# Message passes: the last tile's two matmuls on 64 rows each, its second feature half and its matrix rows held at the upper partitions too

## The reference, cut to what matters

```python
def _spmm(src, dst, w, x, n):
    return jax.ops.segment_sum(w[:, None] * x[src], dst, num_segments=n)
# layer 0: two of these
agg = _spmm(src, dst, edge_weight, x, n)
h = (x + agg) @ W + b
x = jax.nn.gelu(_layer_norm(h, g, be), approximate=False)
# layer 1: one, with a weight of 1 for each edge, scaled by 1 / sqrt(degree)
msg = h[src] * norm[:, None]
out = jax.ops.segment_sum(msg, dst, num_segments=n_nodes)
```

## Time and profile before

| | us |
|---|---|
| median of 3 executions | 1819.25 |
| lowest, highest | 1815.8, 1825.24 |
| the profiled execution's own time | 1821.75 |
| its span in the profile | 1820.0 |

### The profile page before, as it was taken

How to read it: one execution, slowest core, us unless ns; L and a number is a source line. 1 busy time by engine, 2 the same in 40 slices (tenths; PEclk the granted TensorE clock), 3 DMA queues, 4 the chain that set the end, 5 groups by cost and what they waited for, 6 DMA issues and landing times.

```text
span 1820.0 us, 30944 instructions
## 1 busy us (share of the span) xinstructions
PE 1697.8 (93%) x10117; PEld 1359.8 (75%) x10118; DVE 946.7 (52%) x1613; ACT 569.3 (31%) x854; POOL 187.2 (10%) x263
## 2 busy tenths in 40 slices
PE   6999999888889999999999999999999999998995
PEld 4898888888776777777777777766677777787784
DVE  7999999998873301111034444643413143345446
ACT  3135677788890000000011111234400000004442
POOL 4000000000001100000000000000000000153683
PEclk9999999999999999999999999989999999999998
DMA  4103344454459544445434434900064434434375
GB/s 98 1 23 135 135 165 187 200 214 202 196 239 352 166 146 142 138 148 162 146 117 121 127 121 122 242 36 1 18 207 152 135 108 126 144 122 130 105 243 180
DMA packets 136919, 261.73 MB, mean 144 GB/s; under 512 B 22236, under 2 KB 74735, under 8 KB 136606
## 3 DMA queue, kind: packets, MB, share of 16 engines
q1 hardware_dynamic: 116824, 237.02, 40.2%
q0 software_dynamic: 5808, 14.70, 2.2%
q10 hardware_dynamic: 14230, 9.29, 1.7%
HBM read 161.13 MB, written 108.09 MB: 148 GB/s over the span
## 4 chain that ended last, share of the span: by engine, by line
issue 56%; PE 29%; ACT 7%; DVE 4%; ACTq 1%; POOL 1%; DMA 1%; DVEq 1%; SPq 0%; POOLq 0%
PE ps L2143 12%; PE ps L2174 6%; ACT wide L878 4%; PE ps L2144 4%; ACT ps L822 3%; PE ps L2395 2%; PE ps L2379 2%; DVE act_c L1385 1%; PE ps L2042 1%; PE ps L2387 1%; PE ps L2371 1%; ACTq L865 0%; PE ps L2191 0%; PE ps L2203 0%; ACTq L822 0%
## 5 line engine op out<-in xcount | busy, mean ns | idle before, releaser
L2174 PE MATMUL ps<-wide 128*128 128x320 f32 (+1 forms) x2000 | 533.2, 427 | 0.0
L2174 PEld LDWEIGHTS ps<-wide 128*128 128x128 f32 x2000 | 378.3, 190 | 141.3 <-ACT act_c L1001 0.3
L2143 PE MATMUL ps<-early,act_c 128*128 128x200 bf16 x2400 | 299.3, 254 | 46.7 <-ACT ps L822 30.2
L2143 PEld LDWEIGHTS ps<-early,act_c 128*128 128x128 bf16 x2400 | 222.7, 98 | 61.6 <-issue 60.0
L2174 PE MATMUL ps<-wide,act_a 128*128 128x320 f32 (+1 forms) x1000 | 264.4, 426 | 2.3 <-ACTq L910 1.7
L2174 PEld LDWEIGHTS ps<-wide,act_a 128*128 128x128 f32 x1000 | 189.8, 190 | 75.6 <-DMA wide<-weight_matrix 2.1
L878 ACT COPY wide<-ps 128x832 f32<-128x832 f32 x200 | 169.8, 849 | 131.5 <-PE ps L2144 129.7
L822 ACT ACTIVATE ps<-wide 128x832 f32 (+1 forms) x200 | 173.4, 868 | 40.6 <-ACT wide L878 33.3
L1385 DVE TENSOR_TENSOR act_c<-act_a,pair_tab 128x3072 bf16<-128x3072 bf16 x98 | 169.8, 1752 | 21.3 <-PE ps L2144 21.3
L1513 DVE TENSOR_TENSOR wide<-ps,rows 128x1280 f32<-128x1280 f32 x10 | 14.9, 1490 | 283.5 <-PE ps L2191 283.5
L2143 PE MATMUL ps<-act_a,act_c 128*128 128x200 bf16 x1152 | 140.4, 251 | 13.5 <-issue 7.1
(11 more groups left out here) (264 smaller groups left out, 1794.7 us busy)
## 6 DMA issues: line engine op xcount, KB each, us to landing
wide<-weight_matrix SPq DMA_DIRECT2D x90, 800.0 KB, 4.5
wide<-count_matrix SPq DMA_DIRECT2D x45, 800.0 KB, 4.5
weight_matrix<-wide SPq DMA_DIRECT2D x60, 480.0 KB, 2.5
count_matrix<-wide SPq DMA_DIRECT2D x60, 480.0 KB, 2.6
weight_matrix<-wide SPq DMA_DIRECT2D x20, 560.0 KB, 2.7
count_matrix<-wide SPq DMA_DIRECT2D x20, 560.0 KB, 2.7
wide<-weight_matrix SPq DMA_DIRECT2D x20, 400.0 KB, 3.8
routed_tokens<-in_x_dram SPq DMA_DIRECT2D x2, 3072.0 KB, 28.6
```

What stands on the lines that cost most here:

```text
L2143: nc.tensor.matmul(weights, hot_parts[:, slot % PART_SLOTS, part, two, :, k], hot_key[mask_slot][:, mask_two, 0:WCOLS, k], start=False, st ...
L2174: i = nc.tensor.matmul(ps[:, 2 * sub + h, 0:n], features[:, q * QUADS + t, h * P:(h + 1) * P], moving, start=q == 0 and t == 0, stop=q == ...
```

## The change

In tile 24 only the lower 53 rows hold nodes, so 64 rows are enough for a matmul. For this tile the matmul h = 0 now uses partitions 0 to 63, and h = 1 uses partitions 64 to 127. For that the second feature half of tile 24 must lie at partitions 64 and up too (`double_tail`, a DMA within SBUF issued by ACT, 53 rows of 512 bytes, once for each pass), and the tile's 64 matrix rows are written twice to DRAM (`TAIL_ROWS`, two more DMAs by SP for each unit and matrix, 64 rows of 640 bytes each), which makes the four pieces 6 tiles each. PE gets one more wait in each pass, ahead of the first sub-block's last tile. A semaphore is saved by joining `moe_w1_loaded` and `moe_w2_loaded`.

```diff
-PIECES = (slice(0, 7), slice(7, 13), slice(13, 19), slice(19, 25))
-STORED = 16 * len(PIECES)
+HALF_ROWS = P // 2
+PIECES = (slice(0, 6), slice(6, 12), slice(12, 18), slice(18, 24))
+TAIL_ROWS = (slice(0, HALF_ROWS), slice(HALF_ROWS, P))
+STORED = 16 * (len(PIECES) + len(TAIL_ROWS))
...
# SP, write(u2, half, n)
                 sp.dma_start(matrix[ds(u2, 1), half, :, tiles, :].rearrange("a p t c -> (a p) t c"),
                              stage[half][:, first_row + tiles.start:first_row + tiles.stop, :]).then_inc(written[half], 16)
+                if tiles.stop == TILES - 1:
+                    for part in TAIL_ROWS:
+                        sp.dma_start(matrix[ds(u2, 1), half, part, TILES - 1, :].rearrange("a p c -> (a p) c"),
+                                     stage[half][0:HALF_ROWS, first_row + TILES - 1, :]).then_inc(written[half], 16)
...
# ACT, after the weight loads and the waits behind them
+            def double_tail(features):
+                act.dma_start(features[HALF_ROWS:HALF_ROWS + LAST, TILES - 1, P:D], features[0:LAST, TILES - 1, P:D]).then_inc(tail_doubled, 16)
+
             def take_sums(k, s, sub):
...
+            act.wait_ge(input_normed, UNITS)
+            double_tail(act_a)
             super_blocks(act, first_layer, gelu_first)
+            act.wait_ge(gelu_done, 1 + SUPERS)
+            double_tail(act_b)
...
             gcn_operand(SUPERS - 1)
+            act.wait_ge(gcn_in, SUPER + SUPERS * SUPER)
+            double_tail(act_b)
...
# PE, stream(k, s, sub, q)
                 for t in range(QUADS):
+                    tail = q == UNITS - 1 and t == QUADS - 1
+                    if tail and first_block:
+
+                        pe.wait_ge(tail_doubled, 16 * (k + 1))
                     for h in range(KD):
-                        moving = ring[:, q, :, t, :] if n == SUB else last_ring[:, q, t, 0:n]
-                        i = nc.tensor.matmul(ps[:, 2 * sub + h, 0:n], features[:, q * QUADS + t, h * P:(h + 1) * P], moving,
-                                             start=q == 0 and t == 0, stop=q == UNITS - 1 and t == QUADS - 1)
+                        part = slice(h * HALF_ROWS, (h + 1) * HALF_ROWS) if tail else slice(0, P)
+                        moving = ring[part, q, :, t, :] if n == SUB else last_ring[part, q, t, 0:n]
+                        i = nc.tensor.matmul(ps[:, 2 * sub + h, 0:n], features[part, q * QUADS + t, h * P:(h + 1) * P], moving,
+                                             start=q == 0 and t == 0, stop=tail)
```

More of the change, by code:

```diff
@@ L88 @@
 HALF = UGROUPS // 2
-PIECES = (slice(0, 7), slice(7, 13), slice(13, 19), slice(19, 25))
-STORED = 16 * len(PIECES)
+HALF_ROWS = P // 2
+PIECES = (slice(0, 6), slice(6, 12), slice(12, 18), slice(18, 24))
+TAIL_ROWS = (slice(0, HALF_ROWS), slice(HALF_ROWS, P))
+STORED = 16 * (len(PIECES) + len(TAIL_ROWS))
+assert LAST <= HALF_ROWS and PIECES[-1].stop == TILES - 1
 ACCS = 8
@@ L482, in build_program @@
         input_normed = sem("input_normed")
+        tail_doubled = sem("tail_doubled")
         degree_sums = sem("degree_sums")
@@ L508, in build_program @@
         gcn_in = sem("gcn_in")
-        moe_w1_loaded = sem("moe_w1_loaded")
-        moe_w2_loaded = sem("moe_w2_loaded")
+        moe_weights_loaded = sem("moe_weights_loaded")
         biases_loaded = sem("biases_loaded")
@@ L726, in _ @@
                         here_e = slice(e * D, (e + 1) * D)
-                        sp.dma_start(moe_w1[:, :, here_e], a["L1_ffn_w1"][e].rearrange("(k p) n -> p k n", p=P)).then_inc(moe_w1_loaded, 16)
-                        sp.dma_start(moe_w2[:, :, here_e], a["L1_ffn_w2"][e].rearrange("(k p) n -> p k n", p=P)).then_inc(moe_w2_loaded, 16)
+                        sp.dma_start(moe_w1[:, :, here_e], a["L1_ffn_w1"][e].rearrange("(k p) n -> p k n", p=P)).then_inc(moe_weights_loaded, 16)
+                        sp.dma_start(moe_w2[:, :, here_e], a["L1_ffn_w2"][e].rearrange("(k p) n -> p k n", p=P)).then_inc(moe_weights_loaded, 16)
                     sp.dma_start(moe_b1, a["L1_ffn_b1"].rearrange("e n -> (e n)").partition_broadcast(P)).then_inc(biases_loaded, 16)
@@ L2354, in _ @@
             message_pass(2, [0])
-            pe.wait_ge(moe_w1_loaded, 16 * MOES)
-            pe.wait_ge(moe_w2_loaded, 16 * MOES)
+            pe.wait_ge(moe_weights_loaded, 16 * 2 * MOES)
             def experts_at(first, parts):
```

## The result

The changed kernel takes 1845.32 us (median of 4 executions, 1840.96 to 1851.3) against 1819.31 for the kernel before in the same comparison: 26.0 us more. The ratio is 1.0145, 95% interval 1.012 to 1.0169. The forecast was 1840 in a range of 1829 to 1852.

A forecast was written before the change was run, and what follows sets the result against it. PE, busy for 93% of the span, was taken to bound the kernel. Profiled 1821.75 + 22.3 (wait) + 2.5 (clock) - 4 (halves) = 1842.5; that execution was 2.5 above the median, so 1840 us, range 1829 to 1852.

The forecast's parts named there:

- The spacing and the clean path: In a pass, time is PE's instructions times spacing (0.269 us at 320 columns); any added wait stays in full.
- The wait in pass 0: Before the first last tile PE waits for the copy behind ACT's weight loads: 22.3 us, bounds 19 to 29.
- 2.6 to 5.9: Bounds in us for landing pass 0's copy: a write in quiet, or the router's loads just ahead of it.
- The clock: After PE's stand in pass 0, 5 us at 1.2 GHz, half of it lost: 2.5 us, bounds 0 and 5.
- The halves beside each other: Last tiles' row halves run beside each other: 0.15 us saved per wide tile, 4 us over all 30.
- in sequence: Rival: last tiles' halves run one after the other, 12 us lost, 1856 with the stall; 8 in 100.
- strict program order: Rival: last tiles' records start strictly in program order, three slots for a tile, 8 us more, 1848; 8 in 100.
- switching isn't free: Last tiles: two switches cost 0.39 us; the rival, free switching with the stall, gives 1828, 7 in 100.
- The copies of passes 1 and 2: Free: features complete 14 us (pass 1) and 10 us (pass 2) before the last tile; uncovered, 3 to 6 each.
- The writes of stage 1: 80 more DMAs, 30 us of SP's queue, hidden by 419 us of SP waiting for ACT's copies: no cost.

The follow-up runs named there:

- the run on the same rows: Kernel before with the last tile's two matmuls both on partitions 0 to 63, no copies, waits or other writes: 1859.54 us, 1.006 times before.
- the wait alone: Kernel before with only the three copies and PE's three waits for them, last tile still on 128 rows: 1874.76 us, 1.0133 times before.
- the run with the copy by SP: Changed kernel with pass 0's copy issued by SP, ahead of its second sub-block loads, instead of by ACT: 1855.95 us, 1.0037 times the kernel before.
- the writes alone: Kernel before with six DMAs instead of four for each unit and matrix, nothing else: 1858.79 us, 1.0061 times before.
- x loaded twice: Changed kernel with x's last 53 rows loaded to partitions 0 and 64 instead of pass 0's copy and wait: 1854.92 us, 1.0023 times the kernel before.
- five DMAs: The kernel before with split writes only, the last tile's 128 rows in one DMA, five for each unit and matrix: 1854.59 us, one execution.
- the loads doubled: Kernel with x loaded twice, matrices written as before, SP loading the last tile's lower 64 rows twice into the ring: 1844.92 us, 0.997 times the kernel before.

## Why the prediction came out

**The spacing and the clean path** held: what was added to PE's queue in pass 0 stayed in full: 24.2 us until the record behind `degrees(0)` and none of it given back in the pass. In pass 2 it doesn't hold, as the run on the same rows shows (2.0 us of 3.9): the waits of the earlier trace rows end at 838, and PE has others there.

**The wait in pass 0** was the decisive step, and right in place, cause and size: 22.3 us forecast, 22.68 measured, 22.91 with the wait alone. Its terms: ACT free at 597.3 forecast, 600.5 measured. 2 us of that is the start of the loads (560.26; 558.3 forecast), from the later stage 1. The loads themselves took 40.3 us, 2.2 less than before, where 3.5 were forecast: a standing PE does free ACT's queue, by less. Since PE too came to its last tile 2.6 us late, the stand came out the same. That its size is right to 0.4 us is in part luck: the landing was forecast for 600.7 and came at 603.84, and the later stage 1 moved both its ends. The copy took 1.20 to issue and landed 3.0 after its issue began; 0.4 and then 3 were forecast. That a mere move to another queue would have met a new backlog (12.0 us to land) the prediction's "2.6 to 5.9" did not contain; the run with the copy by SP showed it.

**The clock** cost 1.7 us, 2.5 were forecast from a restart whose slow stretch lasted 5 us; here it lasted 3.5.

**The halves beside each other** were forecast from pairs of 64 columns, at 0.15 us for each tile; it is 0.14 to 0.145. The rivals fell on the record list: the halves start 0.007 us apart, so they neither run in sequence nor in strict program order, and the first record behind each switch comes 0.36 us after the one before it, so switching isn't free. The run on the same rows measured the two switches alone, 0.39, as worked out from the earlier trace rows. The rule of the Trainium skill (TensorEngine Tiling, Key Properties), that a change of tiling mode drains the engine, agrees with the 0.36 us here. Of its "up to 2x" 1.08 us against 0.93 is left, with 0.39 us for the two switches.

**The copies of passes 1 and 2** were free, as forecast: in the changed kernel neither pass shows a wait for one.

**The writes of stage 1** were the step that was mis-sized: "They are hidden by 419 us in which SP waits for ACT's copies" priced them at 0, and they cost 2.5 to 3.4 us ahead of the passes in the four kernels with six DMAs, while the other kernels with four begin the passes from 0.2 us earlier to 0.7 later than the kernel before. The cover named, SP's idle time and ACT's landing waits, was there and held; the loss isn't in a wait for SP or for a landed write, and so neither view of the earlier trace rows could show it. There is a second part, ACT's weight loads, which took 46.9 to 47.2 us in the writes alone, with x loaded twice and with five DMAs, and 42.5 to 43.6 in the kernels with four that don't stand. With it the writes alone come to 7.9 us in the trace and 10 in the medians. The changed kernel has not this part: ACT's loads are out before the copy is issued, they took 40.3 us beside a standing PE, and no wait for the degree sums is left. So the wait alone (26 us), the writes alone (10) and the halves (-4) don't add up to the change (26), while 26 + 3 - 4 = 25 comes near.

The sum in place of the forecast's 20.8: 22.7 + 1.7 + 2.6 - 4 = 23.0. The medians give 26.0, with an interval of 22 to 31 us; 3 us stay unassigned and are within it. So the mechanism of the forecast is what ran, and the term at fault is the one for the writes.

## What to carry to other kernels

A small DMA has the delay of its place: of everything ahead of it in the instruction queue that issues it, and of the backlog of the DMA queue that it goes to. Before adding a wait to the engine that bounds the kernel, find the issuing engine's timeline at that moment; here 26.5 KB cost 24 us because 40 us of weight loads stood in front, and x and the ring loaded twice delayed nothing that the trace shows (first message matmul at 551.45, before at 551.67). Packing two half-height matmuls pays only what the two switches leave, here 0.14 of 0.54 us, so such a change has to be free of every other cost, the doubled data's included: put those where the machine has slack (loads in a pass), not where it has none (writes in a stage in which PE is busy for 396 us and DVE for 424 of 444).

## What the runs showed that was not expected

- More and smaller DMAs that nobody waits for slowed a stage of PE, DVE and ACT work: 28% more packets (25024 instead of 19584 from 72 to 516 us, the same 69.6 MB, in the changed kernel) and 2.4 to 3.4 us more in 478, in all four kernels with six DMAs for each unit and matrix.
- While two DMA queues were both loaded, the weight loads of one took 47.0 us in place of 42.5 in the kernel with the writes alone; from 560 to 600 us the other queue moved 3661 packets there (10.66 MB) and 3187 before (10.20 MB). The packets are not what decides: with the loads doubled it moved 3746 (10.26 MB), and the weight loads took 43.6 us.
- A copy of 26.5 KB within SBUF landed after 3.0 us from a queue that had nothing left but small loads, and after 12.0 us from one with a backlog of large writes.
- A wait of 3.9 us cost PE as much by the clock behind it (5.7 us at 0.50) as one of 22.7 us, or more (3.5 us at 0.50).
